# Input products of the second recurrence made beside attention, and a body's states held in PSUM

## Time and profile before

| what | value |
|---|---|
| time before, median of 3 runs | 617.13 us (614.12, 617.13, 618.78) |
| profiled execution: its own time, its span | 613.99 us, 612.1 us |
| mean granted TensorE clock in it | 0.992 |
| busy share of the span: PE, DVE, ACT, POOL | 93%, 86%, 70%, 33% |
| first step of body 0, of body 24, of body 25, last step | 113.0, 451.0, 469.4, 589.7 us |

### The profile page before, as it was taken

How to read it: one execution, slowest core, us unless ns; L and a number is a source line. 1 busy time by engine, 2 the same in 40 slices (tenths; PEclk the granted TensorE clock), 3 DMA queues, 4 the chain that set the end, 5 groups by cost and what they waited for, 6 DMA issues and landing times.

```text
span 612.1 us, 29176 instructions
## 1 busy us (share of the span) xinstructions
PE 571.5 (93%) x11514; PEld 469.6 (77%) x11514; DVE 524.4 (86%) x2325; ACT 430.7 (70%) x2258; POOL 202.6 (33%) x426
## 2 busy tenths in 40 slices
PE   6888787999999999999999999999999999999972
PEld 2555454788888888888888888888889988998862
DVE  6789886799888889899989999999767788899985
ACT  5587775477777777777777777777758677777764
POOL 1556464011000001110111111011100599898886
PEclk9999999899999999999999999999999999999997
DMA  6000000000000000000000000000020000000001
GB/s 219 2 2 1 2 2 1 3 4 4 4 3 4 3 4 3 4 4 4 4 4 4 4 3 3 4 3 4 3 73 2 3 20 17 20 16 20 16 19 31
DMA packets 8632, 8.35 MB, mean 14 GB/s; under 512 B 944, under 2 KB 7088, under 8 KB 8496
## 3 DMA queue, kind: packets, MB, share of 16 engines
q1 hardware_dynamic: 8208, 5.51, 3.0%
q10 hardware_dynamic: 288, 0.99, 0.5%
HBM read 3.35 MB, written 2.10 MB: 9 GB/s over the span
## 4 chain that ended last, share of the span: by engine, by line
PE 63%; POOL 23%; issue 9%; DVE 2%; DMA 1%; ACT 1%; POOLq 0%; SPq 0%; DVEq 0%
PE PS L1479 20%; PE PS L1529 15%; POOL prob_lo L448 4%; PE PS L1490 4%; POOL r_dev L516 4%; PE PS L1500 4%; POOL ln_small L526 3%; PE PS L1431 2%; PE PS L1438 2%; PE PS L1432 2%; PE PS L1494 2%; PE PS L1486 2%; POOL k L539 2%; POOL k L502 2%; POOL ln_small L530 2%
## 5 line engine op out<-in xcount | busy, mean ns | idle before, releaser
L637 ACT ACTIVATE y<-PS 128x16 f16<-128x16 f32 x512 | 94.3, 184 | 132.3 <-PE PS L1494 121.4
L1529 PE MATMUL PS<-ballast,ident 128*128 128x245 f16 (+7 forms) x648 | 142.7, 296 | 0.0
L1041 DVE TENSOR_TENSOR y_lo<-ys,y 128x16 f16<-128x16 f32 x512 | 96.5, 188 | 49.1 <-ACT ys L638 38.8
L1479 PE MATMUL PS<-y_lo,res_hi 128*128 128x8 f16 x2048 | 128.0, 168 | 2.3 <-DVE y_lo L1041 1.1
L1479 PE MATMUL PS<-y,res_hi 128*128 128x8 f16 x2048 | 127.4, 168 | 0.2
L1479 PEld LDWEIGHTS PS<-y,res_hi 128*128 128x128 f16 x2048 | 96.8, 96 | 38.8 <-ACT y L637 19.0
L1479 PE MATMUL PS<-y,res_lo 128*128 128x8 f16 x2048 | 123.4, 166 | 0.0
L453 POOL TENSOR_TENSOR small<-small,minus_half 128x2 f32<-128x2 f32 x32 | 25.6, 799 | 295.2 <-DVE y_lo L1041 260.3
L638 ACT ACTIVATE ys<-PS 128x16 f32<-128x16 f32 x512 | 99.1, 194 | 0.0
L640 ACT ACTIVATE kp<-PS 128x16 f32<-128x16 f32 x512 | 97.5, 190 | 0.0
L1479 PEld LDWEIGHTS PS<-y_lo,res_hi 128*128 128x128 f16 x2048 | 87.9, 96 | 5.5 <-DVE y_lo L1041 3.2
(11 more groups left out here) (240 smaller groups left out, 1483.8 us busy)
## 6 DMA issues: line engine op xcount, KB each, us to landing
ys<-in_x SPq DMA_DIRECT2D x8, 256.0 KB, 7.6
out<-gate_all SPq DMA_DIRECT2D x24, 64.0 KB, 1.5
mats<-in_mats ACTq DMA_DIRECT2D x1, 709.0 KB, 5.0
h_last<-h_all SPq DMA_DIRECT2D x4, 128.0 KB, 2.7
gate_last<-gate_all SPq DMA_DIRECT2D x4, 128.0 KB, 2.9
out<-gate_last SPq DMA_DIRECT2D x16, 32.0 KB, 1.9
rows<-in_rows ACTq DMA_DIRECT2D x1, 257.5 KB, 7.5
wall<-in_wall SPq DMA_DIRECT2D x1, 256.0 KB, 4.8
```

Of the source, the lines that this page charges most:

```text
L637: a_.activation(y16[:, :].rearrange("p (m b) -> p m b", m=NH), pre, ACT.Tanh, scale=back).then_inc(y16_ready, 1)
L1041: v.tensor_tensor(y_lo[:, :], ys[:, :, bass.ds(i * STEPS + (1 + t), 1)].rearrange("p n o -> p (n o)"), y16[:, :], ALU.subtract).then_inc(l ...
L1479: t_.matmul(dst[:, m, :], wts[:, k, m * P:m * P + P], st[:, k * B:k * B + B], start=False, stop=False, skip_group_check=True)
L1529: t_.matmul(at[:, 0:size], ident16[:, :], ballast[:, 0:size], start=False, stop=True, skip_group_check=True)
```

## The change

1. **Input products move.** PE makes them for a whole tile (both halves of 128 states, two products) in `drive(j)`: at t = 6 of bodies 4 to 23 for tiles 11 to 30, at t = 10 of bodies 4 to 14 for tiles 0 to 10, at t = 15 of body 23 for tile 31. They stand in place of that step's `pads`. ACT copies the 128x256 result out of bank 7 into SBUF (`take_drive`): at t = 7 of the same body, at t = 2 of the next body, and at t = 0 of body 24. PE's `feed` is gone from bodies 24 to 31. DVE's `feed_scaled` and `recur` now read and write the products in SBUF.
2. **States of bodies 25 to 30 are held.** ACT writes the full-precision tanh into bank 6 or 7 of PSUM (`HELD`), DVE's `y_lo` reads it there, and at t = 2 of the next body ACT copies all 256 columns into `ys` (`keep_states`). DVE's sums of the last quarter wait for that (`states_kept`).
3. The product with 112 zero columns (L1490) is issued in bodies 25 to 31 as well, in none of body 24.
4. Storage: the products of tiles 0 to 7 lie where `h_last` and `gate_last` will be, so SP's move of the last quarter waits for the first 16 rows of the second recurrence; those of tiles 28 to 31 lie in `mats`.

The diff, without the declarations of semaphores:

```diff
@@ -156,8 +156,10 @@
 z_all = sb("z_all", [P, NT])
-h_last = sb("h_last", [P, B, P])
-gate_last = sb("gate_last", [P, B, P])
+last = sb("last", [P, NH, B, P])
+h_last, gate_last = last[:, 0, :, :], last[:, 1, :, :]
+drives = sb("drives", [P, NH, 2 * B + B // 2, P])
+late_drives = mats[:, 0:B * P].rearrange("p (m k n) -> p m k n", m=NH, n=P)
@@ -337,6 +343,30 @@
 FED_EARLY = STEPS - 4
+
+def is_held(i):
+    return FIRST_READ <= i < BODIES - 1
+
+FIRST_DRIVE = 4
+LATE_DRIVE = FIRST_DRIVE + AHEAD - 2
+
+def drives_of(j):
+    q, b = j // B, j % B
+    if q == 0:
+        return last[:, :, b, :]
+    if j < NT - B // 2:
+        return drives[:, :, j - B, :]
+    return late_drives[:, :, b - B // 2, :]
+
+def drive_count(j):
+    return 2 * j + 2 if j < LATE_DRIVE else 2 * (j - LATE_DRIVE) + 1 if j < 2 * LATE_DRIVE else j + 1
+
+def early_drive(i):
+    return i - FIRST_DRIVE if FIRST_DRIVE <= i < FIRST_DRIVE + LATE_DRIVE else None
+
+def late_drive(i):
+    j = i + AHEAD - 2
+    return j if LATE_DRIVE <= j < NT - 1 else None
 assert IN_SCAN == SPLIT
@@ -382,6 +412,7 @@
     sp.wait_ge(h_ready, NT)
+    sp.wait_ge(ssm_done, B * NH + EIGHT_FREE)
     for half in range(2):
@@ -635,8 +666,11 @@
         a_.activation(y16[:, :].rearrange("p (m b) -> p m b", m=NH), pre, ACT.Tanh, scale=back).then_inc(y16_ready, 1)
-        a_.activation(ys[:, :, bass.ds(i * STEPS + (1 + t), 1)].rearrange("p (m b) o -> p m (b o)", m=NH), pre,
-                      ACT.Tanh, scale=back).then_inc(acted, 1)
+        if is_held(i):
+            state = HELD[i % 2][:, t, :].rearrange("p (m b) -> p m b", m=NH)
+        else:
+            state = ys[:, :, bass.ds(i * STEPS + (1 + t), 1)].rearrange("p (m b) o -> p m (b o)", m=NH)
+        a_.activation(state, pre, ACT.Tanh, scale=back).then_inc(acted, 1)
         a_.activation(kp[:, :].rearrange("p (m b) -> p m b", m=NH), pre, ACT.Copy, scale=keep_scale
@@ -686,11 +720,19 @@
     act.reg_load(keep_scale, setup[0:1, 24:25].bitcast(I32))
+    def take_drive(j):
+        act.wait_ge(drive_made, drive_count(j))
+        a_.activation(drives_of(j), DRIVE.rearrange("p (m n) -> p m n", m=NH), ACT.Copy).then_inc(drive_taken, 1)
+
     for i in range(FIRST_DECAY):
...
                 gate_half(i)
+            if t == 2 and early_drive(i - 1) is not None:
+                take_drive(early_drive(i - 1))
+            if t == 7 and late_drive(i) is not None:
+                take_drive(late_drive(i))
             if (t, i) == (7, 17):
@@ -745,12 +787,21 @@
         scan(t, FIRST_DECAY, FIRST_DECAY % REGIONS)
+        if t == 0:
+            take_drive(NT - 1)
         if t >= 2:
             decay(t - 2)
+    def keep_states(i):
+        act.wait_ge(acted, (i + 1) * STEPS)
+        a_.activation(ys[:, :, 1 + i * STEPS:1 + (i + 1) * STEPS].rearrange("p n t -> p t n"), HELD[i % 2], ACT.Copy
+                      ).then_inc(states_kept, 1)
+
     act.wait_ge(k_cols_free, 1)
...
             scan(t, i, i % REGIONS)
+            if t == 2 and is_held(i - 1):
+                keep_states(i - 1)
             if i == FIRST_READ and t < 2:
@@ -1038,7 +1089,8 @@
         dve.wait_ge(acted, n)
-        v.tensor_tensor(y_lo[:, :], ys[:, :, bass.ds(i * STEPS + (1 + t), 1)].rearrange("p n o -> p (n o)"), y16[:, :],
+        state = HELD[i % 2][:, t, :] if is_held(i) else ys[:, :, bass.ds(i * STEPS + (1 + t), 1)].rearrange("p n o -> p (n o)")
+        v.tensor_tensor(y_lo[:, :], state, y16[:, :],
                         ALU.subtract).then_inc(lo_ready, 1)
@@ -1154,10 +1206,12 @@
         dve.wait_ge(sigma_ready, (FULL - B + n // NH) * NH + NH + ROWS_FREE)
+        dve.wait_ge(states_kept, BODIES - 4 - FIRST_READ)
         last_sums(n, 0, HALF, sigma_half)
...
         dve.wait_ge(sigma_half, n + 1)
+        dve.wait_ge(states_kept, BODIES - 2 - FIRST_READ)
         last_sums(n, HALF, THIRD, sigma_third)
@@ -1258,6 +1312,9 @@
+    def drive_row(s, c):
+        return drives_of(half_q(c) * B + c % 2 * 4 + s % 4)[:, s // 4, :]
+
     def feed(s, c):
@@ -1266,8 +1323,8 @@
     def feed_scaled(s, c):
-        dve.wait_ge(ssm_fed, c * 8 + s + 1)
-        fed = PS[:, 6 + s % 2, 0:P]
+        dve.wait_ge(drive_taken, drive_count(half_q(c) * B + c % 2 * 4 + s % 4))
+        fed = drive_row(s, c)
         if half_q(c) == NQ - 1:
@@ -1278,15 +1335,16 @@
         dve.wait_ge(ssm_done, n - 7 + EIGHT_FREE)
+        fed = drive_row(s, c)
         first = ssm[:, m, half_q(c), (c % 2) * 4 * P + k * P + P - 1:(c % 2) * 4 * P + k * P + P]
         if half_q(c) == NQ - 1:
-            v.tensor_tensor_scan(row[:, 0, :], row[:, 0, :], PS[:, 6 + s % 2, 0:HALF], first, ALU.mult, ALU.add
+            v.tensor_tensor_scan(row[:, 0, :], row[:, 0, :], fed[:, 0:HALF], first, ALU.mult, ALU.add
                                  ).then_inc(ssm_halved, 1)
             dve.wait_ge(ssm_halved, n - 8 * 2 * (NQ - 1) + 1)
-            v.tensor_tensor_scan(row[:, 1, :], row[:, 1, :], PS[:, 6 + s % 2, HALF:P], row[:, 0, HALF - 1:HALF], ALU.mult, ALU.add
+            v.tensor_tensor_scan(row[:, 1, :], row[:, 1, :], fed[:, HALF:P], row[:, 0, HALF - 1:HALF], ALU.mult, ALU.add
                                  ).then_inc(ssm_done, 1)
         else:
-            v.tensor_tensor_scan(row, row, PS[:, 6 + s % 2, 0:P], first, ALU.mult, ALU.add).then_inc(ssm_done, 1)
+            v.tensor_tensor_scan(row, row, fed, first, ALU.mult, ALU.add).then_inc(ssm_done, 1)
@@ -1307,6 +1365,7 @@
                 dve.wait_ge(sigma_third, n_row + 1)
+                dve.wait_ge(states_kept, BODIES - 1 - FIRST_READ)
                 last_sums(n_row, HALF + THIRD, THIRD, sigma_last)
@@ -1485,7 +1544,7 @@
                   skip_group_check=True)
-        zeros = 112 if i < FIRST_DECAY else 0
+        zeros = 112 if i != FIRST_DECAY else 0
         if zeros:
@@ -1528,8 +1587,31 @@
+    def drive(j):
+        b, q = j % B, j // B
+        pe.wait_ge(b_t_ready, 1)
+        if drive_count(j) > 1:
+            pe.wait_ge(drive_taken, drive_count(j) - 1)
+        pe.wait_ge(xn_ready, j + 1)
+        for m in range(NH):
+            one = t_.matmul(DRIVE[:, m * P:m * P + P], b_t[:, m * P:m * P + P], xn[:, b, 1 + q * P:1 + q * P + P],
+                            start=True, stop=True, skip_group_check=True)
+        one.then_inc(drive_made, 1)
+
     def pads(t, i):
         j = i + AHEAD
+        if t == 6 and late_drive(i) is not None:
+            pe.wait_ge(gate_raw, late_drive(i) + 1)
+            drive(late_drive(i))
+            return
+        if t == 10 and early_drive(i) is not None:
+            pe.wait_ge(gate_raw, j - 1)
+            drive(early_drive(i))
+            return
+        if t == 15 and j == NT:
+            pe.wait_ge(gate_raw, NT)
+            drive(NT - 1)
+            return
         tile, early, fill_at = j < NT, j <= NT, i % REGIONS < 2 and t in (4, 5, 8, 9)
@@ -1552,6 +1634,8 @@
                 pe.wait_ge(gate_raw, j - 1)
+                if late_drive(i) is not None:
+                    pe.wait_ge(drive_taken, drive_count(late_drive(i)))
                 for n in range(2 if fill_at else 4):
@@ -1663,13 +1747,6 @@
-    def feed(s, c):
-        m, k = s // 4, s % 4
-        pe.wait_ge(ssm_done, c * 8 + (s - 1) + EIGHT_FREE)
-        t_.matmul(PS[:, 6 + s % 2, 0:P], b_t[:, m * P:m * P + P],
-                  xn[:, (c % 2) * 4 + k, 1 + half_q(c) * P:1 + half_q(c) * P + P],
-                  start=True, stop=True).then_inc(ssm_fed, 1)
-
     def spread_delta(n):
@@ -1722,7 +1799,6 @@
     pe.wait_ge(pv_done, NA * NT)
-    pe.wait_ge(b_t_ready, 1)
     pe.sem_inc(k_cols_free, 1)
@@ -1731,8 +1807,6 @@
         spread_delta(2 * t + 1)
-        if t >= 4:
-            feed((t - 4) % 8, (t - 4) // 8)
     for i in range(FIRST_READ, BODIES):
@@ -1743,9 +1817,6 @@
                 pe.wait_ge(decayed, 2 * 2 * NQ)
-            f = FED_EARLY + (i - FIRST_READ) * 8 + t // 2
-            if t % 2 == 0 and f < 8 * 2 * NQ:
-                feed(f % 8, f // 8)
             body_readouts(readout, t, i)
```

More of the change, by code:

```diff
@@ L196, in build @@
         MISC = PS[:, 7, :]
+        HELD = [PS[:, 6 + n, 0:STEPS * NH * B].rearrange("p (t n) -> p t n", t=STEPS) for n in range(2)]
         SPREAD = MISC[:, 288:292]
+        DRIVE = MISC[:, 512 - NH * P:512]
         wall_loaded = sem("wall_loaded")
@@ L272, in build @@
         ssm_zeroed = sem("ssm_zeroed")
-        ssm_fed = sem("ssm_fed")
+        states_kept = sem("states_kept")
+        drive_made = sem("drive_made")
+        drive_taken = sem("drive_taken")
         ssm_scaled = sem("ssm_scaled")
```

## The result

The changed kernel takes 639.81 us (median of 6 runs, 637.67 to 641.09) where before has 614.58 (6 runs, 613.78 to 618.78): ratio 1.0391, 95% interval 1.0355 to 1.0426. It is 25 us slower, outside the forecast's range, and no rival had reached it. (The forecast was built on 617.13, the median of three of these six runs of before; the median of all six is 614.58. In changes, +0.7 us was forecast and +25.2 measured.) The profiled execution of after took 637.67 us with a span of 635.8; the span of before was 612.1, so 23.7 us have to be found.

A forecast was written before the change was run, and what follows sets the result against it. POOL was taken to bound the read phase, the PE-ACT-PE step circle the attention bodies. Terms +4.0 - 2.5 - 0.8 + 0 = +0.7 on 613.99 gave 614.7; 3.1 to the runs' median made 617.8 us, range 611.5 to 623.

The forecast's parts named there:

- Part 2: Bodies 26 to 31: 2.0 us less POOL waiting against 1.9 more from SBUF contention, net 0, bounds -2.8 and +5.
- Part 1a: Products beside attention on PE, bodies 4 to 23: drives outlast the pads they replace and lengthen steps, +4.0 us.
- the first rival: Pads not tight and SBUF port not contended: a drive may cost what the pads did, 611 us; chance 0.17.
- the third: Drives are cheap but POOL keeps the read phase as long: -2.0 us, 615; chance 0.14.
- what a drive takes more: A drive's 0.53 us against the replaced pads' 0.42 at t = 10 or 0.40 at t = 6 lengthens the step.
- +6.9 bound: Upper bound for the drives beside attention, if each paid 0.31 us twice: 32 x 0.09 more.
- Part 1b: ACT's copies of the products out of PSUM: covered by PE's half of the step, 0 us.
- Part 1c: Feeds gone from body 24: twelve at 0.22 us, less 0.1 kept by ACT's floor, -2.5 us, body at 15.9.
- Part 1d: Eight feeds gone from body 25, less the added zero product: -0.8 us, bounds 0 and -1.8, body at 16.5.
- The forecast's other sign: In the read phase, the profile would show DVE's y_lo never above 0.25 us.
- The slow rival: DVE holds up POOL's four blends in the read phase, 0.28 us a tile: total +6.4, 624 us; chance 0.15.

The follow-up runs named there:

- e1_clock: The changed kernel with 512 filler columns on PE ahead of both reads of every tile; 621.46 us (10 runs), ratio 1.0091.
- e9: The kernel before with PE's input products of the second recurrence taken away, all else kept; 626.67 us (one run).
- e12: The changed kernel with superfluous waits ahead of drives left out and 256 filler columns ahead of the reads of tiles 4 to 23; 617.69 us (6 runs), ratio 1.0060.
- e2: The changed kernel without held states, ACT writing every state straight to SBUF; 641.07 us (one run).
- e6_trimmed: The changed kernel with 512 filler columns ahead of both reads of every tile and already implied waits ahead of drives left out; 615.98 us (one run).

## Why the prediction was wrong

**The missing step.** Part 2 said that removing the feeds "relieves PE by 0.24 a tile, but PE isn't the floor" and priced it at nothing. What stood unsaid under it was that PE would keep its full clock with less to do, and that failed: the granted clock went to 0.50. The runs put a price on what was left out: 123.23 - 105.92 = 17.3 us of the 23.7 come back when PE gets filler in place of the feeds (e1_clock), and taking the feeds alone from before costs 17.4 in the same bodies (120.42 - 102.98, e9). The earlier trace rows held half of a warning: PE, though not the floor, was busy for 96.66 of 102.98 us, more than POOL, so it had no room for a lower clock. The kernel's own text held the other half: a helper named `keep_clock` puts filler ahead of the reads of tiles 0 to 3 and from 24 on. None of the rivals, the slower one included, had the clock in it, so the range could not reach.

**Part 1a, the drives, mis-sized: +4.0 forecast, +7.2 measured.** The mechanism was right: no slack behind the pads, every excess lengthens the step, at t = 6 to 1.12 us where 1.00 was forecast and at t = 10 to 1.07 where 0.98 was (the first rival, "pads were not tight", and the third, cheap drives, are refuted). The drive's own 0.53 was right too (0.52). What failed is "what a drive takes more": the four waits ahead of it cost 0.11 more than two (0.18 against 0.07), which neither the working nor the +6.9 bound held. Without the superfluous ones the bodies take +3.6, close to the 4.0.

**Part 1b, the copies: 0, right.** ACT's copy takes 0.40 us at t = 2 and 7, and in bodies 4 to 22 no step but the drives' is longer by more than 0.01 us than in before.

**Part 1c, body 24: -2.5 forecast, -2.4 measured**, at the 15.9 us that the text named. e9's 15.91 shows that it is the feeds.

**Part 1d, body 25: -0.8 forecast, -0.3 measured** (17.02 in place of 16.5). It lies within its bounds, but its terms were off, by one run each: taking the feeds alone gives 0.5 (e9, 16.82) where the working had 0.9; the change without held states is at 17.27 (e2), so the zeros and the rest cost 0.45 where 0.2 was taken, and held states, not in this term, give 0.25.

**Part 2, the SBUF port: 0 forecast, at full clock +1.7 measured** (e12, 104.65 against 102.98), within -2.8 and +5. In the prediction's own terms: POOL's operations take 3.4 us more (95.89 against 92.51) where 1.9 was forecast, and its waits for ACT fall by 1.7 (from 2.8 to 1.1) where 2.0 was.

```profile
POOL r_var L544 <- ACT k L770: 1.1, 4, 0.6
```

So the gain was sized right and the cost too small. The forecast's other sign came true as well: y_lo, up to 0.48 us in before, is never above 0.18 in bodies 26 to 30. The slow rival had this mechanism, at 0.28 us a tile where POOL's 3.4 us are 0.14; its cause carries about 2 of the 23.7 us.

The sum on the corrected steps: +7.2 - 2.4 - 0.3 + 20.25 in bodies 26 to 31 - 1.0 for the start and the tail = 23.7. Of the 20.25 the clock has 17.3 (by e1_clock) to 18.6 (by e12), and the rest is what the read phase loses at full clock.

## What to carry to other kernels

Before work is taken off TensorE, count the removed matmuls as something that may be holding its clock, also where another engine sets the pace: if PE is nearly as busy as that engine, a half clock makes it the floor. PE's busy time doesn't settle it in advance (before kept its clock through 3.85 of 5 us, e9 lost it after 4.69), so try the removal alone and look at the clock's row first. If such work must go, put filler in its place; here two products of 256 columns a tile held the clock that two feeds had held. Semaphore waits that are already fulfilled still take time on an engine that has no slack: leave out those that an earlier wait implies.

## What the runs showed of the hardware

- TensorE's clock went to its lower level, 1.2 GHz of 2.4 (granted 0.50), after PE had been busy for 4.56 of 5 us in after and 4.69 in e9, while before kept 2.4 GHz through a window with 3.85. In after it stayed low for about 100 us although PE was then busy for 5.00 of 5. The Trainium skill, "TensorE: Matmul & The Clock Gate", Part 1, says that the chip sets this clock by how busy the engine has been; that it fell when work was taken off PE agrees, and by what measure of busy, no run here shows. That the clock may stay low for 100 us on an engine which the low clock itself makes fully busy was not what I expected. What brought it back in body 31, where the reads have filler again, was not tried by itself; in e2_no_held it came back for 10 us in body 29, without filler.
- At that level, in bodies 27 to 29, PE's f32 products of 129 columns took 451 ns (292 at full clock), and its 8-column products 168 to 180 (166 to 168): small products hardly feel the clock.
- Four fulfilled semaphore waits ahead of a matmul put 0.18 us between its start and that of the one before; two put 0.07, and one 0.03 (rows of e6_trimmed, body 12).
- A recurrence of 128 columns on VectorE whose two inputs both lie in SBUF took 579 ns on average beside GpSimd, and 461 with one of them in PSUM; GpSimd's 128x128 blend took 506 and 453.
